# Softmax totals inverted before they are spread, and filler matmuls on TensorE, in a two-layer transformer kernel on one core

## The reference, cut to what matters

```python
x = x + 0.5 * ffn(layernorm(x), ternary weights)      # x: 16 sequences x 256 x 128
x = x + attention_0(layernorm(x))                     # without a softmax
x = x + 0.5 * ffn(layernorm(x), the same weights)
x = x + 0.5 * moe(layernorm(x))                       # 2 of 8 experts, chosen by token 0
x = x + attention_1(layernorm(x))
x = x + 0.5 * moe(layernorm(x))

# attention_1: 16 heads of 8, causal, rotary positions
scores = einsum('bhqd,bhkd->bhqk', q, k) * scale
attn = softmax(where(causal, scores, -inf), axis=-1)
out = einsum('bhqk,bhkd->bhqd', attn, v)
return einsum('dv,bsv->bsd', W_O, out)
```

## Time and profile before

| | us |
|---|---|
| median of 3 runs (lowest to highest) | 767.94 (765.27 to 769.16) |
| the profiled execution's own time | 768.91 |
| its span, first to last instruction | 765.8 |
| busy in the span: PE, PEld, DVE, ACT, POOL | 656.6, 468.1, 524.9, 504.1, 311.3 |

### The profile page before, as it was taken

One profiled execution on the slowest core, in us unless ns is written; L12 is line 12 of the kernel. 1 busy time (PEld: TensorE's weight loads), 2 busy tenths in 40 slices (PEclk: granted clock), 3 DMA queues, 4 the chain that ended last, 5 costly groups with the idle time before them and its releaser, 6 DMA issues.

```text
span 765.8 us, 13407 instructions
## 1 busy us (share of the span) xinstructions
PE 656.6 (86%) x4878; PEld 468.1 (61%) x4878; DVE 524.9 (69%) x1306; ACT 504.1 (66%) x830; POOL 311.3 (41%) x433
## 2 busy tenths in 40 slices
PE   2889989999999998999999897877778778888673
PEld 1667766787777787777787774544445445545442
DVE  3745465677657755677678659988799867879342
ACT  2867677977689858878778952365545666655541
POOL 2200121143423130225345467566747665446432
PEclk9989999999999999999999998699889998989785
DMA  9100000000110000000111123134444353431111
GB/s 296 42 1 1 0 1 1 0 1 2 42 41 1 0 1 1 1 0 1 42 42 42 42 114 113 51 118 144 136 138 136 132 192 118 144 126 58 56 57 29
DMA packets 47083, 47.21 MB, mean 62 GB/s; under 512 B 3240, under 2 KB 41128, under 8 KB 46760
## 3 DMA queue, kind: packets, MB, share of 16 engines
q1 hardware_dynamic: 47016, 46.33, 18.2%
HBM read 23.51 MB, written 22.54 MB: 60 GB/s over the span
## 4 chain that ended last, share of the span: by engine, by line
PE 50%; DVE 17%; ACT 12%; DMA 8%; issue 6%; SPq 4%; POOL 2%; POOLq 0%; DVEq 0%; ACTq 0%
PE PSA L769 15%; PE PSA L773 14%; DMA LC<-do 5%; DVE MX L1070 5%; ACT PSA L1122 3%; PE PSA L935 2%; SPq L1316 2%; PE PSA L786 2%; DVE LC L1091 2%; DVE G L993 2%; DMA QS<-dq 2%; PE PSA L882 2%; ACT G L1118 2%; PE PSA L875 2%; ACT ah L1129 1%
## 5 line engine op out<-in xcount | busy, mean ns | idle before, releaser
L1216 POOL TENSOR_TENSOR RS<-VE,MHALF 128x4 f32<-128x4 f32 x48 | 49.3, 1027 | 228.6 <-DVE VE L975 228.4
L769 PE MATMUL PSA<-ah,WH 128*128 128x512 f32 x320 | 131.8, 412 | 9.0 <-DVE al L998 4.8
L1070 DVE TENSOR_REDUCE MX<-PSA 128x6 f32<-128x768 f32 x128 | 117.2, 945 | 16.3 <-PE PSA L904 16.3
L773 PE MATMUL PSA<-al,WH 128*128 128x512 f32 x320 | 125.9, 393 | 0.0
L1122 ACT ACTIVATE PSA<-PSA,SC 128x512 f32<-128x512 f32 x128 | 84.7, 661 | 55.4 <-PE PSA L773 54.8
L1198 ACT ACTIVATE PB<-PSA 128x768 f32<-128x768 f32 x128 | 99.0, 818 | 16.1 <-PE PSA L922 15.9
L769 PE MATMUL PSA<-bh,WH 128*128 128x512 f32 x256 | 104.7, 409 | 4.8 <-DVE al L998 1.7
L773 PE MATMUL PSA<-bl,WH 128*128 128x512 f32 x256 | 100.2, 392 | 0.0
L1264 POOL TENSOR_SCALAR_AFFINE_SELECT PB<-PB 128x512 f32<-128x512 f32 x128 | 79.8, 635 | 45.2 <-ACT PB L1198 43.6
L998 DVE TENSOR_TENSOR al<-PSA,ah 128x512 fp32r<-128x512 f32 x64 | 44.2, 691 | 67.0 <-ACT ah L1129 67.0
L769 PEld LDWEIGHTS PSA<-ah,WH 128*128 128x128 f32 x320 | 60.5, 189 | 27.0 <-DVE al L998 7.1
(11 more groups left out here) (120 smaller groups left out, 1355.9 us busy)
## 6 DMA issues: line engine op xcount, KB each, us to landing
do<-OT SPq DMA_DIRECT2D x15, 512.0 KB, 4.7
KS<-dk SPq DMA_DIRECT2D x32, 192.0 KB
QS<-dq SPq DMA_DIRECT2D x32, 192.0 KB
dk<-CB SPq DMA_DIRECT2D x16, 192.0 KB, 2.3
dq<-CB SPq DMA_DIRECT2D x16, 192.0 KB, 2.5
X<-in_x SPq DMA_DIRECT2D x8, 256.0 KB, 6.9
dk<-CB SPq DMA_DIRECT2D x16, 128.0 KB, 1.9
dq<-CB SPq DMA_DIRECT2D x16, 128.0 KB, 1.9
```

Of the source, the lines that this page charges most:

```text
L769: e.matmul(o, WH[:, col:col + 128], hi, start=first, stop=False)
L773: return e.matmul(o, WH[:, col:col + 128], low, start=False, stop=last)
L1070: e.tensor_reduce(MX[:, u % 2, :, :].rearrange("p t (l g) -> p l t g", l=2)[:, :, :, g], PSA[:, b:b + 2, 0:384].rearrange("p l (t k) -> p ...
L1216: e.tensor_tensor(RS[:, i, :], VE[:, i, :], MHALF[:, :], ALU.pow).then_inc(g_rs, 1)
```

## The change

For units 0 to 13 the totals are read once for each head and query before they are spread: `tot_in` reads row 8 of do (16 KB) into a tile TOT of 128x32, `inverse` inverts that on VectorE, `tot_out` writes it to a new memory tensor di, and `vl_in` reads LC from di with each of the 16 rows repeated for 8 partitions. `norm_out` then waits for `vl_in` alone. Unit 14 keeps `recip`. For this the memory tensor do has its rows ahead of its head index: `ot_out` writes it in another arrangement, VC comes from one piece of 128 KB, and the rows of W_O and of the selection table are permuted.

`fill` adds matmuls whose result is overwritten (`keep`: 128x128 bf16, the identity with itself) wherever the planner sees TensorE idle: 65% of the planned gap less 0.15 us, at 0.06 us each, into the bank that the plan has free the longest. There are 108 such groups with 756 matmuls. 126 of them stand in the feed-forward part, and 162 stand behind the last `weigh`. They do not move the planner's clocks, so that all other steps' order follows from the new steps of the totals alone.

```diff
-    "vl_in": [("S", 1.12, 1.12), ("D", 3.7)], "recip": [("V", 1.66, 1.74)], "norm_out": [("G", 0.68, 0.72)],
+    "tot_in": [("S", 0.5, 0.5), ("D", 2.6)], "inverse": [("V", 0.28, 0.36)],
+    "tot_out": [("S", 0.5, 0.5), ("D", 2.6)], "vl_in": [("S", 1.12, 1.12), ("D", 3.7)], "recip": [("V", 1.66, 1.74)], "norm_out": [("G", 0.68, 0.72)],
...
+FILLED = 0.65
...
+            if eng == "P":
+                self.fill(s0)
+                self.idle_from = s0 + us
             self.note(eng, s0, s0 + us, name)
             self.clock[eng] = s0 + us
             t = st.at[eng] = s0 + way[0]
         st.done = max([t] + [st.at[e] for e in st.at if name in BESIDE])
         return st
+
+    def fill(self, t):
+
+        free = {b: f for b, f in [*enumerate(self.bank), *self.sr.free.items()] if f}
+        if not free or not self.count.get("mark"):
+            return
+        b = min(free, key=lambda b: self.left(free[b]))
+        n = int((t - max(self.idle_from, self.left(free[b]) + 0.06) - 0.15) * FILLED / 0.06)
+        if n > 1:
+            self.note("P", max(self.idle_from, self.left(free[b]) + 0.06), max(self.idle_from, self.left(free[b]) + 0.06) + 0.06 * n, "keep")
+            k = self.count.get("keep", 0)
+            self.count["keep"] = k + 1
+            self.steps.insert(-1, Step("keep", k, x=n, b=b, emptied=free[b]))
 
...
         if u < NB - 1:
             yield from self.until(o.done - 0.5)
+            if u < NB - 2:
+                o = self.put("tot_in", u=u, src=o)
+                yield from self.until(o.done)
+                o = self.put("inverse", u=u, src=o)
+                yield from self.until(o.done - 0.2)
+                o = self.put("tot_out", u=u, src=o)
+                yield from self.until(o.done - 0.5)
             ld = self.put("vl_in", u=u, src=o, emptied=self.vcfree[u % 2])
             self.vcfree[u % 2] = None
-            yield from self.until(ld.done)
-            rc = self.put("recip", u=u, src=ld)
-            on = self.put("norm_out", u=u, src=rc)
+            yield from self.until(ld.done - 3.0 * (u == NB - 2))
+            if u == NB - 2:
+                ld = self.put("recip", u=u, src=ld)
+                yield from self.until(ld.done - 0.2)
+            on = self.put("norm_out", u=u, src=ld)
...
-        DO = nc.dram_tensor("do", [NB, 4, 32, 4, S], F32)
+        DO = nc.dram_tensor("do", [NB, 32, 4, 4, S], F32)
+        DI = nc.dram_tensor("di", [NB, 4, 4, S], F32)
...
+                elif st.name == "keep":
+
+                    w.wait_ge(g_c, 4)
+                    emptied(w, st.emptied)
+                    for _ in range(st.x):
+                        e.matmul(PSA[:, b, 0:128], IDB[:, :], IDB[:, :], start=True, stop=True)
...
+                elif st.name == "inverse":
+
+                    w.wait_ge(s_tot[u % 2], 16 * (u // 2 + 1))
+                    e.reciprocal(TOT[:, u % 2, :], TOT[:, u % 2, :]).then_inc(v_inv, 1)
...
-                    w.wait_ge(v_rc, st.src.n + 1)
+                    if st.src.name == "recip":
+                        w.wait_ge(v_rc, st.src.n + 1)
+                    else:
+                        w.wait_ge(s_vl[u % 2], 32 * (u // 2 + 1))
                     e.tensor_tensor(VC[:, u % 2, :], VC[:, u % 2, :], LC[:, u % 2, :], ALU.mult).then_inc(g_on, 1)
...
-                    e.dma_start(DO[u].rearrange("v r g t -> (v r) g t"), OT[u % 2][:, :, :]).then_inc(s_dv[u % 2], 16)
+                    e.dma_start(DO[u].rearrange("r v g t -> v r (g t)"), OT[u % 2][:, :, :]).then_inc(s_dv[u % 2], 16)
+                elif st.name == "tot_in":
+                    w.wait_ge(s_dv[u % 2], 16 * (u // 2 + 1))
+                    w.wait_ge(s_inv[u % 2], 16 * (u // 2))
+                    e.dma_start(TOT[:, u % 2, :], DO[u, 8].rearrange("v g (a b) -> (v g a) b", b=32)).then_inc(
+                        s_tot[u % 2], 16)
+                elif st.name == "tot_out":
+                    w.wait_ge(v_inv, st.src.n + 1)
+                    e.dma_start(DI[u].rearrange("v g (a b) -> (v g a) b", b=32), TOT[:, u % 2, :]).then_inc(
+                        s_inv[u % 2], 16)
                 elif st.name == "vl_in":
                     w.wait_ge(s_dv[u % 2], 16 * (u // 2 + 1))
                     for s in st.emptied:
                         w.wait_ge(p_proj, s.n + 1)
-                    for T, r in ((VC, 0), (LC, 8)):
-                        e.dma_start(T[:, u % 2, :], DO[u, :, r:r + 8, :, :].rearrange(
-                            "v r g t -> v (r g) t")).then_inc(s_vl[u % 2], 16)
+                    e.dma_start(VC[:, u % 2, :], DO[u, 0:8].rearrange("r v g t -> (r v g) t")).then_inc(
+                        s_vl[u % 2], 16)
+                    if st.src.name == "tot_out":
+                        w.wait_ge(s_inv[u % 2], 16 * (u // 2 + 1))
+                        totals = DI[u:u + 1].rearrange("o v g t -> o (v g) t").to_broadcast([8, 16, S])
+                    else:
+                        totals = DO[u, 8:16].rearrange("r v g t -> r (v g) t")
+                    e.dma_start(LC[:, u % 2, :], totals).then_inc(s_vl[u % 2], 16)
...
-    arrays["wo"] = w["L1_attn_W_O"].T[np.arange(128).reshape(4, 4, 8).transpose(1, 2, 0).reshape(-1)]
+    arrays["wo"] = w["L1_attn_W_O"].T[np.arange(128).reshape(4, 4, 8).transpose(2, 1, 0).reshape(-1)]
```

More of the change, by code:

```diff
@@ L141, in __init__ @@
         self.table = self.pe = ""
+        self.idle_from = 0.0
         self.lay()
@@ L643, in build @@
         LC = sb("LC", [128, 2, S])
+        TOT = sb("TOT", [128, 2, 32])
         SEL = sb("SEL", [128, 8, 128])
@@ L656, in build @@
         s_vl = [sem(f"s_vl{u}") for u in range(2)]
+        s_tot = [sem(f"s_tot{u}") for u in range(2)]
+        s_inv = [sem(f"s_inv{u}") for u in range(2)]
+        v_inv = sem("v_inv")
         s_out, s_sel, p_spread, v_on = sem("s_out"), sem("s_sel"), sem("p_spread"), sem("v_on")
@@ L1408 @@
     sel = np.zeros((128, 8, 128), f32)
-    sel[32 * v + r, q, 32 * v + 4 * r + q] = 1
-    sel[32 * v + 8, 4 + q, 32 * v + 4 * r + q] = 1
+    sel[32 * v + r, q, 16 * r + 4 * v + q] = 1
+    sel[32 * v + 8, 4 + q, 16 * r + 4 * v + q] = 1
     arrays["sel"] = sel
```

## The result

| | median us | lowest to highest |
|---|---|---|
| before, beside it | 768.55 | 765.27 to 769.71 |
| changed kernel | 791.70 | 789.83 to 793.85 |

The ratio is 1.031, with a 95% interval of 1.027 to 1.035. The change makes the kernel slower by 23 us. I had predicted 763 (747 to 781): wrong in sign, and outside the range. The profiled execution took 793.85 us, its span 791.8.

A forecast was written before the change was run, and what follows sets the result against it. It took VectorE as the engine to relieve in attention_1, where none is full. From 768.9 us, -12.3 + 10 + 2 + 2.5 - 7 = -4.8 gave 764.1; the profiled execution being 1.0 above the median, 763 us, range 747 to 781.

The forecast's parts named there:

- the wait at the inversion: VectorE waiting for TOT before inverting in attention_1: 20 us against 10.1, so +10 us, between -10 and +50.
- SyncE, GpSimd: SyncE's 28 more DMAs and waits for the inversion and di's landing delay what is behind: +2 us, 0 to +8.
- Spreading: Write of do, outermost memory dimension 4: it would get 4 of 16 DMA engines, a share of 0.25.
- Its length: Write of do: 5.3 us in place of 1.3, landing after 6.6 us alone; load on four engines 85%.
- What is behind it: DMA queues: 8 of 14 TOT reads stand behind the four reads or the next unit's write of do.
- VectorE's wait: VectorE at the inversion waits for TOT about 8 times, 2.5 us each, 20 us in all.
- SyncE's wait: SyncE's waits for the inversion and di delay casts, maxima and next reads: +2 us, at most +8.
- The inversion: 14 of 15 inversions on VectorE shrink to 0.35 us each: -12.3 us, between 0 and -19.6.
- What I left at nothing: Reads of VC and LC: together well under 3.3 us expected, but no term of their own in the sum.
- Filler: Filler matmuls in TensorE's gaps: price +2.5 us (0 to +8), gain through the clock -7 us (-14 to 0).
- the four DMA engines: Rival: VectorE stands at the inversion behind do's four-engine write and the reads, 35 us in all: 783 us, chance 0.21.

The follow-up runs named there:

- a_w16: Changed kernel with the write of do cut in four DMAs, one per head index, so that it uses 16 DMA engines: 744.91 us, ratio 0.966.
- b_layout: Kernel before with only the new layout of do (one write on four engines, big inversion kept, no TOT, no filler): 773.39 us, ratio 1.008.
- late_dve: Changed kernel, planner told only the longer landing that VectorE waits for (TOT 6.0 us for 2.6), last spread held: 778.14 us, ratio 1.014.
- late_sp: Changed kernel, planner told only the longer landings that SyncE waits for (do 9.5, di 6.0 us), last spread held: 778.97 us, ratio 1.015.
- b_fill: Kernel before with only the filler matmuls added, no change to the totals: 764.55 us, ratio 0.996.
- a_late: Changed kernel, planner told landings near the measured ones (do 9.5, TOT, di, VC and LC 6.0 us), last spread held: 767.55 us, ratio 0.999.
- a_w16_nofill: Changed kernel with do written in four DMAs on 16 engines and without the filler matmuls: 753.17 us, ratio 0.979.

## Why the prediction was wrong, point by point

**The sum failed at the term for the slow write: "the wait at the inversion" and "SyncE, GpSimd".** I had +12 us for both. With its four-engine write the changed kernel takes 46.8 us more than with a write on 16, so these terms were 35 us short. The rest of the sum gave -16.8 us (-12.3, +2.5 and -7), and a_w16 lies 22.9 under the kernel before, 6 us better; the two make up the miss of 29 us.

- *Spreading.* The new write runs on four engines, share 0.21: right. The Trainium skill, DMA: Bandwidth & Descriptors, "Why a DMA increments its semaphore by 16 and not by 1", gives 4 for this shape; the trace agrees.
- *Its length, mis-sized.* I took 5.3 us, a quarter of the rate on 16 engines, and a landing 6.6 us after the issue. It is 8.3 us and 10.2 (b_layout, alone). One engine moved 24.6 GB/s in the write before (393 / 16) and 16 in this one (64 / 4): I changed the number of engines and kept the rate of each from a write in another layout. The row on four engines, VC and LC at 76 GB/s, gave 6.9 us and would have been the better choice. With 8.3 us for the write, my load for the four engines is 5.5 + 8.3 + 1 = 14.8 us in a unit of 13.9: full, not 85%.
- *What is behind it, missed.* I put only the reads of KS and QS and the write ahead of TOT. But di is written behind the next unit's do as well, and then SyncE waits for di. The small DMAs have 128 rows on both sides, as the write before had that ran at a share of 0.95; if they are on all 16 engines like it, four of theirs are taken. They land after 1.4 us at best, 10.2 in the chain. The Trainium skill, same page, "Queues, rings and completion order", says that descriptors are consumed in ring order on each engine; the trace agrees: 10.21 us for 16 KB behind the write, and a median of 3.0 with the write on 16.
- *VectorE's wait.* 20 us forecast at TOT, 22.0 measured, about 8 times against 7. Right, and taking 13.9 of these away gave back 13.6 us (late_dve). What I left out is unit 14's wait for LC, 7.2 us, where the kernel before had none: in all 19 us more than before (29.2 against 10.1), not 10.
- *SyncE's wait, the failed step.* +2 us, at most +8. SyncE stood 69.9 us, and taking about half of that away (37.0 left, 21.4 + 15.6) gave back 12.7 us (late_sp). I had named what is queued behind these waits, and then priced them by SyncE's small share of the chain before. Nor does their sum price them: SyncE's waits as a whole didn't grow (204.3 to 193.3 us).

**The inversion.** 0.35 us each, as predicted. -12.3 us forecast for it; with a fast write the small one is worth 9.6 us, the price of its two more trips taken off (762.8 to 753.2). Right in kind and near in size.

**What I left at nothing.** The faster reads of VC and LC, with the write cut in four and kept on 16 engines, are worth 6.2 us (769.0 to 762.8).

**Filler.** In the first 430 us nothing moved by more than 1 us: right. Net I had -4.5 us; the runs show -3.3 on the kernel before, -8.3 on the fast write, and nothing in the changed kernel. There the clock in attention_1 is 0.88 with filler as it was without in the earlier trace rows. The planner fills gaps that it foresees, and the waits for DMAs are not among them, as I had said. In the end the clock rose from 0.57 to 0.94, but the gain of 3 us didn't come. From the last inversion to the end of the span it is 24.5 us before, 24.1 after and 22.8 in b_fill, by these rows:

```profile
L1097 DVE RECIPROCAL LC<-PSA x1: 1757/1757/1757, 741.3 to 741.3; 128x256 f32<-128x256 f32 x1
```

```profile
L1140 DVE RECIPROCAL LC<-PSA x1: 1758/1758/1758, 767.7 to 767.7; 128x256 f32<-128x256 f32 x1
...
776.44 1.17 PE PSA L945 x11
```

```profile
L1121 DVE RECIPROCAL LC<-PSA x1: 1758/1758/1758, 740.0 to 740.0; 128x256 f32<-128x256 f32 x1
```

The second row of the changed kernel is from its chain: a group of filler lay on the path, 1.17 us.

**The rivals.** The second one, "the four DMA engines", is what happened: VectorE at the inversion, SyncE behind. It gave 783 at 35 us of VectorE's waits. The mechanism was right, but its place was not: VectorE's waits for TOT stayed at 22 us, under the 25 that I named as its turning point (29.2 with unit 14's), and SyncE's decided as much. I gave it 0.21 since I took the load as 85%, which rests on the 5.3 us.

**Still open.** Why each engine is slower in the new layout of do, and how four DMAs on the same four engines gain 17 us; how much of a_late's 24 us its filler gave; and whether the 1.8 us of filler in the changed kernel are a cost or nothing.

## What to carry to other kernels

Before a layout in memory is turned, look at what it does to the outermost dimension of every DMA that touches it, and price the lost engines for all that is queued behind, small transfers first: 16 KB behind the write took 10.2 us here, 1.4 at best. Don't carry one engine's rate over from another layout either. A planner's table must have the landing under load: with the same slow DMAs, the order made for them gave back 24 us of the 47, its filler included. A chain of small trips through memory multiplies one slow transfer: the same write cost 10.6 us with one trip behind it and 36.7 with three.

## What the runs showed of the hardware that I had not expected

- A write of 512 KB with 4 KB pieces ran at 24.6 GB/s for each engine in the old layout and at 14 to 16 in the new one, on 16 engines (228 GB/s) as on four (64 GB/s, 53 to 57 in its first stretches). Cut in four DMAs with 1 KB pieces, on the same number of engines, it ran at 80 in a stretch of 1.2 us.
- A read of 192 KB with an outermost dimension of 8 in place of 6 raised the rate from 142 to 191 GB/s, about in proportion, by the order of two names in one line. It was worth 7.2 us of 769.
- The mean clock is a poor guide to time: b_fill went from 0.931 to 0.968 for 3.3 us, a_w16 against a_w16_nofill from 0.943 to 0.976 for 8.3.
